# A two-stage graph network on one core: attention and attribute sampling put in another order

## What is computed

```python
def sage(h, Wself, Wneigh, b):                 # twice, relu between
    mean = segment_sum(h[src], dst) / maximum(deg, 1)
    return h @ Wself + mean @ Wneigh + b
x = layernorm(x + sage(relu(sage(x, ...)), ...))
# attention over edges, 4 heads of 128
q, k, v = x @ Wq + bq, x @ Wk + bk, x @ Wv + bv;  e = edge_attr @ We + be
alpha = einsum(q[dst], k[src] + e) / sqrt(128)
attn = softmax of alpha over the edges of one dst
agg = segment_sum((v[src] + e) * attn, dst)
out = agg + x @ Wskip + bskip
lin = (layernorm(out) * ln_g + ln_b) @ Wlin + blin
x = layernorm(x + elu(lin + x))
```

## Time and profile before

| | us |
|---|---|
| median of 3 runs | 1707.49 |
| lowest, highest | 1705.91, 1707.91 |
| the profiled execution | 1708.48 |
| its span | 1706.6 |

### The profile page before, as it was taken

How to read it: one execution, slowest core, us unless ns; L and a number is a source line. 1 busy time by engine, 2 the same in 40 slices (tenths; PEclk the granted TensorE clock), 3 DMA queues, 4 the chain that set the end, 5 groups by cost and what they waited for, 6 DMA issues and landing times. The chain is left out here.

```text
span 1706.6 us, 34140 instructions
## 1 busy us (share of the span) xinstructions
PE 1520.9 (89%) x7749; PEld 1023.4 (60%) x7749; DVE 1315.2 (77%) x6172; ACT 1168.3 (68%) x3146; POOL 1029.6 (60%) x1038
## 2 busy tenths in 40 slices
PE   4999999999999997998788858999999999999872
PEld 3777777777777776887455533555555555555441
DVE  5999999999999996665466645777777777777761
ACT  2999999999999994443365633666666666666662
POOL 2888888778888864772555525555555555555220
PEclk9999999999999998999799989999999999999995
DMA  3667666644444442332588843322223332333110
GB/s 75 148 154 163 152 160 157 157 147 152 145 149 148 149 142 63 97 90 63 186 270 268 270 130 95 85 81 83 84 82 84 85 80 84 86 85 85 54 33 5
DMA packets 178392, 205.98 MB, mean 121 GB/s; under 512 B 36561, under 2 KB 104620, under 8 KB 178276
## 3 DMA queue, kind: packets, MB, share of 16 engines
q1 hardware_dynamic: 149656, 166.88, 32.4%
q0 software_dynamic: 27200, 36.26, 9.6%
q10 hardware_dynamic: 1420, 1.60, 0.3%
HBM read 106.69 MB, written 106.49 MB: 125 GB/s over the span
## 5 line engine op out<-in xcount | busy, mean ns | idle before, releaser
L1370 POOL DMA_INDIRECT out_dram<-big,idx x98 | 99.6, 1016 | 256.9 <-DVE big L1686 122.9
L1353 POOL DMA_INDIRECT big<-x_tab,look x196 | 199.5, 1018 | 90.8 <-issue 50.1
L732 PE MATMUL pb<-MG_s,big 128*128 128x256 f32 x832 | 207.4, 392 | 26.5 <-ACT big L765 26.4
L732 PEld LDWEIGHTS pb<-MG_s,big 128*128 128x128 f32 x832 | 149.5, 189 | 128.5 <-ACT big L765 112.4
L741 ACT ACTIVATE big<-big 128x128 f32<-128x128 f32 x416 | 180.2, 482 | 0.0
L714 PE MATMUL pb<-C_s,big 128*128 128x128 f32 x832 | 161.6, 276 | 0.0
L715 PE MATMUL pb<-Ws1c_s,big 128*128 128x128 f32 x832 | 161.6, 276 | 0.0
L1103 POOL DMA_INDIRECT big<-h1e_tab,hidx x98 | 97.6, 996 | 103.2 <-PE pb L982 46.2
L863 POOL TENSOR_TENSOR big<-big,cl 128x512 f32<-128x512 f32 x104 | 133.5, 1284 | 36.8 <-DVE big L837 35.9
L1454 PEld LDWEIGHTS pb<-Wg_s,big 128*128 128x128 f32 x784 | 95.8, 192 | 97.5 <-ACT big L1526 97.1
L905 POOL DMA_INDIRECT look<-redirect,idx x98 | 114.1, 1165 | 29.6 <-issue 27.1
(11 more groups left out here) (351 smaller groups left out, 4055.1 us busy)
## 6 DMA issues: line engine op xcount, KB each, us to landing
big<-in_x_dram SPq DMA_DIRECT2D x104, 256.0 KB, 3.3
x_tab<-big SPq DMA_DIRECT2D x98, 256.0 KB, 2.5
out_dram<-big SPq DMA_DIRECT2D x98, 256.0 KB, 2.1
ve_tab<-c_ve SPq DMA_DIRECT2D x98, 256.0 KB, 2.9
c_ve<-ve_tab SPq DMA_DIRECT2D x98, 256.0 KB, 2.8
h1e_tab<-a_rows SPq DMA_DIRECT2D x25, 256.0 KB, 2.6
x_tab<-a_rows SPq DMA_DIRECT2D x25, 256.0 KB, 2.4
big<-eT_tab SPq DMA_DIRECT2D x98, 64.0 KB, 1.9
```

Source lines behind the costliest of these rows:

```text
L732: t = pe.matmul(o, b_x1T[:, r * P:(r + 1) * P], MG_s[:], start=True, stop=True)
L1353: g.indirect_dma_start(out=o, out_offset=None, in_=x1_tab, in_offset=bass.IndirectOffsetOnAxis(ap=look[:, a, j:j + 1], axis=0), bounds_che ...
```

## The change

In phase c the four attribute products of a step are made in the next step: number 0 after the matrices product, 1 after the attribute transposes, 2 and 3 after L1148. The copies out of PSUM are moved with them on ScalarE and VectorE. There are six buffers `c_ve` (two tiles of phase a are used again). The store of transposed attributes is left out; the load of attributes takes four rows in a run, so a tile holds every fourth edge, and the store of values puts them back in order with rows 8 KB apart. SP issues the stores one by one between its other work.

In phase d the attributes are loaded as they are and transposed by TensorE with the other rows, and ScalarE copies three tiles rather than two. In each softmax function the second scan gets a function of its own (`below`, `whole`) at the end of VectorE's turn. The shares are exp(logit - maximum - ln(sum)): ScalarE takes a logarithm and an exponential, VectorE a subtraction. ScalarE copies the transposed normalised rows before the second norm's logarithm, two of four logits stand before L1680, and VectorE begins its turn with L1648. Some waits that others imply are left out; the small results get two buffers each.

```diff
 def attr_out(eng, copy, s, r):
-            landed_before(eng, dma_vs(t % 4), t // 4)
+            landed_before(eng, dma_vs(t % VR), t // VR)
 ...
 c_pe:
+            def attr_product(s, r):
+                if s >= 0 and r in tiles_of(s):
+                    after(pe, "c_eT", s)
+                    after(pe, f"c_ve{r % 2}", (R * s + r) // 2 - 1)
+                    pe.matmul(VE[r % 2][:], c_eT[s % 2][:, r, :], We_s[:], start=True, stop=True)...
...
+                attr_product(j, 0)
                 [transposes of the attributes of s]
+                attr_product(j, 1)
                 [product with Wn1 of j = s - 1]
-                if s < NG:
-                    after(pe, "c_eT", s)
-                    for r in tiles_of(s):
-                        after(pe, f"c_ve{r % 2}", (R * s + r) // 2 - 1)
-                        pe.matmul(VE[r % 2][:], c_eT[s % 2][:, r, :], We_s[:], ...)
+                attr_product(j, 2)
+                attr_product(j, 3)
 c_act:
+                    from_even(s - 1, 0)          # before the copy of TE
...
-                    for r in tiles_of(s)[0::2]:
-                        attr_out(act, ..., s, r)
+                    from_even(s - 1, 2)
 c_dve:
+                    from_odd(s - 1, 1)           # before L1206
...
-                    attr_out(v, v.tensor_copy, s, 1)
...
-                    attr_out(v, v.tensor_copy, s, 3)
+                    from_odd(s - 1, 3)
 c_sync:
-                    sp.dma_start(c_ea[s % 2][:], edge_attr[...].rearrange("(r p) d -> p r d", p=P)
+                    sp.dma_start(c_ea[s % 2][:], edge_attr[...].rearrange("(p r) d -> p r d", r=R)
...
+                        place = ve_tab[s * BLK:(s + 1) * BLK, :].rearrange("(p r) d -> p r d", r=R)[:, r, :]
...
-                    sp.dma_start(eT_tab[...], c_eT[s % 2][:, 0:n, :])
+                attr_rows(s - 1, 0)
+                if s + 2 < NG:
+                    load(s + 2)
+                attr_rows(s - 1, 1)
                 [store of the normalised rows of s - 2]
+                attr_rows(s - 1, 2)
+                attr_rows(s - 1, 3)
 d_sync:
-                sp.dma_start(d_xT[j % XT][:, 2 * D:3 * D], eT_tab[j * P:(j + 1) * P, :])
+                sp.dma_start(d_ea[j % 4][0:n, :], edge_attr[j * P:j * P + n, :])
 d_pe:
+                    pe.wait_ge(dma_ea[a % 4], 16 * (a // 4 + 1))   # with the waits for the rows
-                    for i, s_ in enumerate((d_x1s[a % 4], d_x1d[a % XD])):
+                    for i, s_ in enumerate((d_x1s[a % 4], d_x1d[a % XD], d_ea[a % 4])):
 d_act:
-                    act.activation(d_xT[a % XT][:, 0:2 * P], TB[:, 0:2 * P], ACT.Copy)
+                    act.activation(d_xT[a % XT], TB[:, 0:3 * P], ACT.Copy)
+                if ends_group(a - 2):            # exponential of the group, was at the end, a - 1
+                    act.activation(g_ex[0:n, :], g_d[0:n, :], ACT.Exp)
+                if ends_group(a - 3):
+                    act.activation(g_r[0:n, :], g_den[0:n, :], ACT.Ln)
...
-                    [L1519, L1521 before L1526]
+                    [L1526 before L1519, L1521]
...
+                if ends_group(a - 3):            # after the output
+                    act.activation(g_at[0:n, :], g_d[0:n, :], ACT.Exp)
 d_dve:
-                v.reciprocal(g_r[0:n, :], g_den[0:n, :])
-                v.tensor_tensor(g_at[0:n, :], g_ex[0:n, :], g_r[0:n, :], ALU.mult)
+                v.tensor_tensor(g_d[0:n, :], g_d[0:n, :], g_r[0:n, :], ALU.subtract)
```

199 lines of the change are left out of this document (107 added, 92 removed).

## The result

The changed kernel takes 1646.76 us (median of 4 runs, 1643.84 to 1648.84) beside 1707.7 us for the kernel before, timed with it (4 runs, 1705.91 to 1708.93): a ratio of 0.9643, 95% interval 0.9625 to 0.966. The forecast was 1650.1 us. The profiled execution has a span of 1644.6 us, before 1706.6.

What follows compares the result with a forecast made beforehand. Bounds: in the edge loop TensorE's wait for ScalarE's PSUM copy, in the attention loop the VectorE-ScalarE chain. Edge -27.5 and attention -29.9 give -57.4 us: from 1707.49 to 1650.1 us, range 1637 to 1676.

Steps and rivals of the forecast that it cites:

- Edge step: Edge loop: a step falls from 7.05 to 5.75 us (bounds 5.65 and 6.1), 28.6 us less over 22 steps.
- (b): Edge loop: POOL's gathers plus a restart set the step at 6.03 us, total 1656.3 us; chance 0.09.
- (d): Edge loop: step stays at 7.05 us, the wait moving to VectorE's copy behind L1202, total 1678.7 us; chance 0.05.
- Start of the loop: First edge steps: the second starts once its gathers land, about 825.6 us; 2 us less (bounds 5 less, 1.5 more).
- (c): Edge loop start: low clock covers the whole second step, 11.4 us instead of about 7.5, total 1653.5 us; chance 0.13.
- The whole edge loop: Edge loop: steps 28.6 us less, start 2 less, end 3.1 more, together -27.5 us.
- Transfers: Edge loop: 1.62 MB in a 5.75 us step, 282 GB/s, 88% busy, below full; striding costed at nothing.
- (e): Edge loop: strided value stores cost 2.7 times as much, steps reach 8.4 us, total 1710 us or more; chance 0.03.
- Attention turn: Attention loop: TensorE sets an ordinary turn at 6.01 us (5.97 to 6.07) instead of 6.15.
- (a): Attention loop: VectorE and ScalarE still set 6.15 us a turn, only softmax is hidden, total 1665.4 us; chance 0.15.
- the copy moved ahead of the pair: Attention loop: ScalarE's copy before the second norm's pair ends the final product's wait, which then takes 0.90 instead of 1.00 us.
- The attention loop: Attention loop: seven-turn groups 1.97 us shorter give -24.8 us, the last ten turns -5.1, together -29.9 us.

Runs made afterwards that it cites:

- e8: Changed kernel with two unread TensorE transposes (0.22 us) added per attention-loop turn: 1716.8 us, ratio 0.9935 to the kernel before.
- e7: Changed kernel with all four logits in one block behind the second norm, as before the change: 1720.13 us, ratio 0.9949 to the kernel before.
- e6: Changed kernel with ScalarE's copy of the transposed normalised rows back behind the second norm's pair: 1706.37 us, ratio 0.9868 to the kernel before.
- e5: Changed kernel unaltered, timed again on a second chip: 1700.45 us beside 1728.39 for the kernel before, ratio 0.9837.
- e10: Changed kernel with four buffers for loaded edge attributes instead of two, loads issued four steps ahead: 1712.43 us, ratio 0.9874 to the kernel before.
- e2: Kernel before with only the new attention loop, its old edge loop kept: 1699.3 us, ratio 0.9809 to the kernel before.
- e1: Kernel before with only the new edge-loop order and six value buffers, old transfers and attention loop kept: 1743.92 us beside 1732.52, ratio 1.0065.
- e12: Changed kernel with two unread wide products (1.73 us) added to each edge step: 1712.42 us beside 1733.01 for the kernel before, ratio 0.9883.
- e9: Changed kernel with edge attribute loads issued by ScalarE instead of SyncE: 1712.56 us beside 1732.54 for the kernel before, ratio 0.9891.
- e3: Changed kernel with attributes loaded in 512 B runs and values stored contiguously, as before: 1710.53 us, ratio 0.9875 to the kernel before.
- e4: Changed kernel with four value buffers instead of six: 1707.14 us, ratio 0.9853 to the kernel before.

## Why the prediction was right, and where it was not

- Edge step, the main term: 5.75 forecast, 5.66 measured on the first chip, which is the sum of TensorE's own work (5.68) with no loss. The caution of 0.09 for narrow margins was not needed; every copy came in time, and between 838 and 958 us the one wait is of 0.27 us for a gather (936.17). Rivals (b), POOL, and (d), VectorE's copy, didn't occur: POOL's gathers follow each other with 0.30 us of issue, and no product waits for L1126.
- Start of the loop: 2 us less forecast. The third matrices product stands at 833.24, where before it stood at 835.64, but 1.3 of these 2.4 us come from ahead of the loop, so the start gained 1.1. The second step started at 824.87, as forecast for the gathers (about 825.6), and took 8.37 us, as the lower clock covered more than half of it. Rival (c), the low clock over the whole second step, with 11.4 us, didn't occur. With the rule that the prediction cites from the Trainium skill, "TensorE: Matmul & The Clock Gate", section Part 1: The HAM clock gate, the trace agrees this far: after the idle time the clock was at its lower level, and it rose while TensorE was at work. It rose some 2 us later than before (828 to 829 us has 0.82 before; 829 to 831 us has 0.69 now); that the new wait of 2.85 us is what delayed it is not shown.
- The whole edge loop, -27.5 forecast, -26.6 measured. From the third matrices product to the last (990.62 before, 958.91 now) it gained 29.3 us (28.6 forecast), at the start 1.1 (2 forecast), and the end, from the last matrices product to the attention loop, got longer by 3.8 (3.1 forecast): 18.3 us before, 22.2 now. Together 26.6 less.
- Transfers: 278 GB/s at a share of 0.88, close to the forecast, but in part by luck: 1.85 MB less one part of seven is 1.58 MB a step, not the 1.62 of the prediction (278 GB/s x 5.66 us gives 1.57), and the shorter step made up for it. The landing of value stores rose from 2.9 to 3.6 us, in the 15 stores for which the trace has it, well inside the 8.6 us that the six buffers leave. Rival (e) is out: with strided stores the step is TensorE's own work. Its price was also worked out wrongly: a store of 256 KB at 0.79 x 16 / 252 costs 13 engine-us, not 10, so it would have had to cost twice as much, not 2.7 times.
- Attention turn: TensorE sets it, as forecast, at 5.95 (5.97 to 6.07 in the working). Line L1481 takes 0.89 once its wait is gone, the lower of the two values that I had weighed. e8 shows the bound directly, and e7 the main reason why VectorE no longer sets it. Rival (a), 6.15 a turn, did not come. The prediction expected equal turns; those with small transposes take 6.06 and 6.32.
- One step was oversold: the copy moved ahead of the pair was said to free L1481. e6 prices it at 3.7 to 5.9 us in the loop, and most turns keep 5.95 without it. It matters only where softmax work of a group lies in the turn.
- The attention loop, -29.9 forecast, -34.1 measured. From the first shares transpose to the last (13 groups) 574.5 us became 545.5, 28.9 less, where the forecast had 24.8 for 12.57 groups: 2.2 us a group, not 1.97, because TensorE's turn came out at 5.95 and not 6.01. Behind the last shares transpose it is 6.1 less (85.5 before, 79.4 now), ahead of the first 0.9 more. For the last ten turns 5.1 less were forecast; the same ten (the prediction's 1601.85 to 1662.44, now 1546.57 to 1603.43) give 60.6 and 56.9, so 3.7 less. Their short turns take 5.37, below the 5.55 assumed, but not all are short. That the total is so near is thus partly luck: a group that gained too much and an end that gained too little.
- What the prediction did not see: its number holds for the session of the first pair. On the one other chip on which the changed kernel itself was timed, it stands at 0.984 in place of 0.964 (e5), and its variants on two more at 0.985 to 0.989. The forecast treated TensorE as having no limit but its instructions' durations, and the trace of before, at 8.0 instructions a microsecond in the edge loop with no lag at all, could not show another. The edge part gives 26.6 us on the first chip and costs 3 to 9 us on the others (191.9 to 198 us, 204.0 in e10, beside 189.2 for the old loop in e2, the only later trace of it), the attention part gives 34.1 and 33.6.

## What to carry to other kernels

Work with the distances of starts: when the sum of one engine's start distances equals the step, that engine is the bound, and only its own work or another engine's added work tells anything more; a pause is filled by moving work of the waiting engine into it, which here was worth 18.4 us (e7), a copy made earlier 5.9 (e6). Before a dense TensorE stream of narrow products is taken as a gain, time it in more than one session and on more than one chip, and check it by the semaphore increments, because TensorE's recorded ends go on when it stands still. When every engine waits for another in a circle and the transfers run dry too, look for the one whose records are modelled.

## What the runs showed of the hardware that was not expected

- In the sessions of e1 to e12, on four chips, TensorE stood still, by its late increments for 4 to 5 us, at about every 250th instruction (waits counted) in the loops that run at 9.8 or 13.8 products and weight loads a microsecond where nothing disturbs them; at 8.6 (e12), with TensorE busy all the time, and at 8.0 (e2) it didn't. At 11.6, in the first phase, the lag was at most 1.5 us and rarer. In the session of the first pair it didn't occur even at 13.8. The cause is not shown.
- Behind five of six such standstills in e5's edge loop the clock was at its lower level, 1.2 GHz (products at 2.05 us in place of 1.02, a mean granted clock of 0.93); in e2's gather phase, with lags of 4.1 us, it stayed at 1.00.
- Adding 42 us of wide products to such a loop lengthened it by 7 to 12 us (e12 beside e9 and e5).
- Stores of 2 KB runs with a stride of 8 KB left the edge step at TensorE's own 5.66 us on the first chip. Where the loop was held up anyway, contiguous stores (with loads of 512 B runs) were no faster on the same chip (e3 197.3 us, e4 196.0).
